# Constant matmuls on TensorE at the start of the MLP and of the FFN

## What is computed

```
mod = (silu(c) @ wmod).reshape(8, 6, 1, 256)
h = layernorm(x) * (1 + ca) + sa
x = x + ga * attn(h)        # Mamba-2 mixer, then an MLP of width 1024 with its own residual
h = layernorm(x) * (1 + cb) + sb
x = x + gb * ffn(h)         # ternary weights: silu(h w1) * (h w2), gelu(. h1), gelu(. h2), w3
```

## Time and profile before

| | |
|---|---|
| median of three runs | 3185.32 us |
| lowest and highest | 3183.98, 3193.42 us |
| the profiled execution's own time | 3180.88 us |
| its span, first to last instruction | 3179.2 us |
| PE matmul busy | 2799.2 us, 88% |
| DVE, ACT, POOL busy | 58%, 44%, 21% |
| mean granted TensorE clock | 0.943 of 2.4 GHz |

### The profile page before, as it was taken

One profiled execution on the slowest core, in us unless ns is written; L12 is line 12 of the kernel. 1 busy time (PEld: TensorE's weight loads), 2 busy tenths in 40 slices (PEclk: granted clock), 3 DMA queues, 4 the chain that ended last, 5 costly groups with the idle time before them and its releaser, 6 DMA issues. The chain is left out here.

```text
span 3179.2 us, 46142 instructions
## 1 busy us (share of the span) xinstructions
PE 2799.2 (88%) x16998; PEld 2086.3 (66%) x16998; DVE 1839.9 (58%) x3504; ACT 1384.6 (44%) x2394; POOL 678.1 (21%) x716
## 2 busy tenths in 40 slices
PE   0488888888888888869999799999999999999999
PEld 0354555455555555458888687887878787878787
DVE  4688888888888888746767433333333333333332
ACT  0566666666666666536555322222222222222221
POOL 5022222222222222210000122222222222222221
PEclk6799989998999899879999899999999999999999
DMA  3010101010101010035211100000000000000000
GB/s 125 29 35 20 35 20 35 20 35 20 35 21 35 21 35 11 28 104 208 70 62 64 48 13 7 11 14 16 14 16 14 16 14 16 14 16 14 16 14 8
DMA packets 104858, 107.06 MB, mean 34 GB/s; under 512 B 35897, under 2 KB 98617, under 8 KB 102977
## 3 DMA queue, kind: packets, MB, share of 16 engines
q1 hardware_dynamic: 99520, 103.81, 10.1%
q10 hardware_dynamic: 5120, 0.19, 0.1%
HBM read 71.41 MB, written 40.94 MB: 35 GB/s over the span
## 5 line engine op out<-in xcount | busy, mean ns | idle before, releaser
L1597 PE MATMUL fbank<-hid,fw 128*128 128x512 f32 x4096 | 962.3, 395 | 0.0
L1597 PEld LDWEIGHTS fbank<-hid,fw 128*128 128x128 f32 x4096 | 766.1, 187 | 187.0
L1747 DVE TENSOR_TENSOR hid<-fhf,hid 128x512 fp32r<-128x512 f32 x384 | 264.9, 690 | 704.3 <-POOL hid L1704 704.3
L1704 POOL TENSOR_SCALAR hid<-fhf 128x512 fp32r<-128x512 f32 x384 | 271.1, 706 | 1040.2 <-ACT fhf L1676 760.8
L808 ACT ACTIVATE mh<-ebank 128x512 f32<-128x512 f32 x512 | 302.0, 598 | 415.0 <-PE ebank L663 413.8
L1121 DVE SCALAR_TENSOR_TENSOR mh<-mh,gm 128x512 f32<-128x512 f32 x512 | 403.2, 794 | 1.8 <-ACT mh L808 1.8
L663 PE MATMUL ebank<-cright,cleft 102*128 102x512 bf16 x512 | 211.1, 413 | 64.1 <-ACT cin L847 28.9
L1676 ACT ACTIVATE fhf<-fbank,sh2c 128x512 f32<-128x512 f32 x128 | 88.0, 688 | 382.4 <-PE fbank L1597 382.4
L676 PE MATMUL yin<-mh,xpad 128*32 128x128 f32 x4096 | 230.5, 300 | 27.1 <-DVE mh L1121 26.6
L650 PE MATMUL ebank<-ah,win 128*128 128x512 f32 x640 | 246.7, 425 | 7.1 <-ACT cin L847 6.6
L1676 ACT ACTIVATE fhf<-fbank,sh1c 128x512 f32<-128x512 f32 x128 | 88.1, 688 | 320.8 <-PE fbank L1597 320.6
(11 more groups left out here) (180 smaller groups left out, 4380.1 us busy)
## 6 DMA issues: line engine op xcount, KB each, us to landing
fx<-x_d SPq DMA_DIRECT2D x17, 512.0 KB, 3.9
xs<-in_x SPq DMA_DIRECT2D x16, 512.0 KB, 4.3
h_d<-in_h SPq DMA_DIRECT2D x16, 512.0 KB, 5.4
o_d<-o SPq DMA_DIRECT2D x16, 512.0 KB, 2.9
mo<-o_d SPq DMA_DIRECT2D x16, 512.0 KB, 3.8
mx<-in_x SPq DMA_DIRECT2D x16, 512.0 KB, 4.8
x_d<-mx SPq DMA_DIRECT2D x16, 512.0 KB, 2.8
fw<-h_d SPq DMA_DIRECT2D x2, 4096.0 KB, 15.2
```

The costliest lines, as they stand in the source:

```text
L1597: mm = pe.matmul(bank[banks.slot(key)][:], w[:, k, m * P:(m + 1) * P].bitcast(dt), h[:, k, :].bitcast(dt), start=(k + n == 0), stop=(k == ...
L1704: pool.tensor_scalar(hid[i % 2][0][:, m, :], hf[j % 3][:], 1.0, 0.0, ALU.mult, ALU.add)\
L1747: dve.tensor_tensor(hid[i % 2][1][:, m, :], hf[j % 3][:], hid[i % 2][0][:, m, :].bitcast(F32), ALU.subtract).then_inc(c_lo.sem, 1)
```

## The change

72 matmuls of ones by ones are put at the head of PE's stream in the MLP, and 72 at the head of PE's stream in the FFN (in both copies of its code). They wait for nothing and signal nothing. Their results go to a bank whose next real use begins with an overwriting matmul.

```diff
+WARM = 72
...
@@ mlp, PE's stream
+            for _ in range(WARM):
+                pe.matmul(acc[0][:, 0:P], ones[:], ones[:], start=True, stop=True)
             transposes(0, 0)
             transposes(0, 1)
             for n in blocks:
...
@@ feed_forward, rows_of_batch
+                for _ in range(WARM):
+                    pe.matmul(bank[0][:, 0:P], ones[:], ones[:], start=True, stop=True)
                 transposes(0, 0)
                 with pe.Fori(0, B) as b:
```

## The result

The changed kernel takes 3199.75 us (median of 10 runs, 3194.52 to 3201.45), the kernel before 3187.73 us (median of 10, 3180.74 to 3194.80). The sum came out; several of its terms did not, and something that the prediction named without a price, the place of the FFN's loop in PE's instructions, is worth more than the whole change.

What follows compares the result with a forecast made beforehand. Once PE has begun the MLP or FFN, nothing else sets its end; late transposes less warm-clock gains gave +4.3 and +6.5 us, together +10.8, so 3196.1 us, with a range of 3188 to 3204.

Steps and rivals of the forecast that it cites:

- The sum: Whole kernel: lateness less gains, +4.3 us in the MLP and +6.5 in the FFN, together +10.8.
- When the constants start, and how long they take: MLP and FFN starts: from 1383.9 and 1797.5, 144 passes at 0.213 then 0.111 us, 18.2 us a burst.
- Lateness of the transposes: MLP and FFN starts: bursts outlast the room of 10.2 and 9.8 us, transposes 8.0 and 8.4 us late.
- The warm clock's gain: MLP and FFN starts: faster transposes and first products give back 3.7 us in the MLP, 1.85 in the FFN.
- so I let it hold: Pauses of the starting chains: the clock stays full through at most 1.6 us (MLP) and some 3.9 us (FFN).
- the fall: Rival: clock falls back in the chain's pause, costing 1.4 us in the FFN, 2.8 in the MLP; chance 0.17.
- the bursts fit: Rival, MLP and FFN starts: single passes make bursts of 10.3 us, gains stand nearly alone, -5.0 us; chance 0.05.
- PE's stream did not run dry: Rival that it would: PE waits for instruction fetches in the bursts, two to four waits, +3.5 to +7 us; chance 0.15.
- the added code may move the loop in the instruction memory: FFN loop: aside in the rival of waits for instruction fetches, chance 0.15; no size of its own.
- The back edge: FFN loop: 1.76 us without a releaser, cited as what a fetch that PE waits for looks like.

Runs made afterwards that it cites:

- gb_after: Changed kernel with the FFN's gate row gb loaded one batch row earlier, into a tile of its own; ratio 0.9990 to the kernel before.
- ffn72: Changed kernel with the MLP's constants removed, leaving 72 in the FFN; ratio 1.0108 to the kernel before.
- both32: Changed kernel with 32 constants in each of MLP and FFN in place of 72; ratio 0.9990 to the kernel before.
- both144: Changed kernel with 144 constants in each of MLP and FFN in place of 72; ratio 1.0123 to the kernel before.
- mlp72: Changed kernel with the FFN's constants removed, leaving 72 in the MLP; ratio 1.0091 to the kernel before.
- mlp80: Changed kernel with 80 constants in the MLP and none in the FFN; ratio 1.0022 to the kernel before.
- short_gb: Changed kernel with 36 constants in the MLP, 32 at the FFN's start, 12 before its first products, gate row gb loaded early; ratio 0.9942 to the kernel before.
- short_only: Changed kernel with 36 constants in the MLP, 32 at the FFN's start, 12 before its first products, gb loaded where it was; ratio 0.9970 to the kernel before.
- gb_before: Kernel before, no constants, with the FFN's gate row gb loaded one batch row earlier into its own tile; ratio 0.9999 to the kernel before.

## Why the prediction was right, and where it was not

**When the constants start, and how long they take: right.** 144 passes in each burst, 17.65 and 18.79 us against 18.2 and a stated 17.5 to 19.0. The clock stayed at 0.50 for the first 2.8 us of the one and 5.2 us of the other; the passes behind that lie 0.112 us apart (forecast 0.111). They start 0.1 us behind the MLP's barrier, not 0.7, for the wait at 1383.9 in the earlier trace rows was not where the stream begins. Lateness of the transposes, from the barrier: 17.6 against 10.9 in the MLP, **+6.7** (forecast 8.0), and 19.5 against 10.6 in the FFN, **+8.9** (forecast 8.4). In gb_after it is 8.3 and 8.4.

**The warm clock's gain: right in the MLP of this execution, wrong in the FFN.** MLP: transposes to first full product 5.11 us against 6.09, -1.0 (forecast 0.9), and no slow products, -2.8. FFN: 4.88 against 5.53, -0.65 (forecast 0.45), but the clock fell at 1828, 3.6 us after the transposes began, and stayed low for 5.5 us of products where it had been 3.1 before: +1.1 instead of -1.4. The step that failed is "so I let it hold". The pause of 3.85 us lay between a pause that had kept the clock and one that had not, and the prediction gave the fall 0.17 and priced it at 1.4 us in the FFN; it cost 2.5, since the slow products lasted longer than before. It fell there in all profiled executions with constants ahead of the FFN's transposes and none behind them (after, ffn72, both32, both144, gb_after). In the MLP it held in the changed kernel's and fell in those of mlp72, mlp80, gb_after, both32, both144, short_gb and short_only, for 3.4 to 6.8 us, though no pause of PE there was longer than 2.7 us; so the whole of the MLP's part of the gain, too, came in one of eight profiled executions. Only the 12 constants inside the FFN's pause held it each time (two executions). Why it fell in the one and held in the other, with the same code, stays open.

**The sum was right with two errors that nearly cancel.** MLP: +6.7 - 1.0 - 2.8 = +2.9, forecast +4.3; measured -0.2, because 3.2 us of waits for mhl went. (With the clock's fall, mlp72 and gb_after have +4.0 and +3.9 there.) FFN: +8.9 - 0.65 + 1.1 = +9.3, forecast +6.5; measured +12.3, with 0.7 more of pauses in the loop, 1.5 for a further fall of the clock in it (3029.6, for 3.4 us) and 0.7 at the end. Together +12.1 in the stages against a forecast of +10.8.

**What went in the MLP.** In blocks 1, 6 and 11 of the kernel before (counted from 0), DVE waits for the tokens of the next block, and PE for DVE. SP issues that load when the store of x_d of the block ahead has landed. The DMA queues around the first of these stores, before and after:

```profile
q8 instruction: 1, 0.02, 1.6%
issues: line engine op xcount, KB each, median us to landing
x_d<-mx SPq DMA_DIRECT2D x1, 512.0 KB, 3.7
```

```profile
x_d<-mx SPq DMA_DIRECT2D x1, 512.0 KB, 2.8
```

Before, one packet of instructions lies in that stretch and the store takes 3.7 us instead of 2.8; after, none does. The other kernels bear this out. Of 180 stores of x_d (15 in each of the twelve profiled executions), 11 have a packet that starts 0.2 to 0.8 us behind the store's issue, and these took 3.3 to 4.6 us to land; the other 169 took 2.8 to 3.2, those with a packet 2.3 us or more behind the issue included. Three of the 11 are in each of before, ffn72 and gb_before, the kernels with no constants in the MLP, and come every fifth block, five blocks being six packets long (5 x 308 instructions are 6.0 x 256). One each is in short_gb and short_only, in a later block, as their 36 constants move the packets by another amount. So the constants changed this by where they put the packets. No run moved a packet alone, but no store in the twelve traces goes against it.

**The rivals.** That the bursts fit was rightly held small: 144 records each. PE's stream did not run dry in the bursts, but the clause "the added code may move the loop in the instruction memory" had the largest effect of the study in it, 29 us of the FFN stage by 32 instructions (mlp72 to mlp80), and was given no price. The back edge stood in the earlier trace rows as 1.76 us without a releaser. The sum held only because 144 constants put the loop at a place where its own pause goes and the wait for gb, until then hidden behind it, takes its room (11.3 us for 11.4): mlp72 and ffn72, each a half of the change, took 29 and 34 us where the same sum gives 4.3 and 6.5. The forecast for the whole was lucky there.

## What to carry to other kernels

Work that fills an idle wait must be counted against the wait, in the passes that the profile has for its type: 72 float32 matmuls were 144 passes and nearly twice as long as the hole. It must also be compared on more than one execution of a stage: the same MLP code with the same 72 constants took 413.3 and 417.5 us. A clock that is warm before a dependent chain need not be warm behind it; here only filler in the last pause before the dense work held it. And an edit that adds or removes instructions ahead of a hardware loop must be compared with a neutral one of the same length: look at the duration of the loop's branch and at pauses without a releaser, then at what is next in line behind them, since here only both together gave the 20 us.

## What the runs showed of the hardware

The branch back of the FFN's loop costs PE's sequencer 3.3 to 3.6 us or 0.2 us by where the loop lies. A row of that loop is 1,647 instructions of PE in the trace, 6.4 packets of 256. In the slow cases they are fetched again in every row, in the cheap ones never: the instruction queue has 60 packets from 1985 to 3165 us before, and none from 1995 to 3185 us after. Its share in 1990 to 2150 us, first before (mlp72 has the same line), then after:

```profile
q8 instruction: 7, 0.11, 0.3%
```

```profile
q8 instruction: 1, 0.02, 0.0%
```

Over the whole execution it is 157 packets before and in gb_before, 158 in mlp72, ffn72 and both32, and 94 to 98 in every kernel with the cheap branch. Places 0, 32, 64 and 128 over a multiple of 256 were tried; where between them the cost changes, and how the length of the loop enters, stays open.
